# Attention and ternary FFN block: row sums of all kv heads taken from exponentials, and down products in seven parts in both passes

## The reference

```python
x = layernorm(x + attention(x, wq, wk, wv, wo))
x = layernorm(x + ffn(x, gate_t, up_t, down_t, gate_s, up_s, down_s))
```

## Time and profile before

| | us |
|---|---|
| median of 3 runs | 1789.99 (1787.49 to 1791.25) |
| the profiled execution | 1786.88 |
| its span | 1785.2 |

### The profile page before, as it was taken

The page is one execution under the profiler, slowest core; times in us unless marked ns, Lnnn a source line. Parts: engine busy times, 40 slices in busy tenths (PEclk is TensorE's granted clock), DMA queues, the critical chain, the costliest instruction groups (busy, mean ns, idle before and its releaser), DMA issues.

```text
span 1785.2 us, 26942 instructions
## 1 busy us (share of the span) xinstructions
PE 1743.6 (98%) x9840; PEld 849.1 (48%) x9840; DVE 1166.6 (65%) x2423; ACT 829.6 (46%) x1675; POOL 462.1 (26%) x813
## 2 busy tenths in 40 slices
PE   8999999999999999999999999999999999999998
PEld 4745564564455434444444444444444444444444
DVE  7997698488758764556544445646657666677456
ACT  6687667566646665365333433441332222231321
POOL 3475456454554652300000002203100000003103
PEclk9999999999999999999999999999999999999999
DMA  8564345234335797477544345558312112132302
GB/s 268 101 137 91 78 119 120 67 101 126 54 84 125 185 213 271 159 256 273 168 174 139 131 161 171 191 159 190 130 62 70 58 66 79 48 110 89 112 12 83
DMA packets 228516, 233.46 MB, mean 131 GB/s; under 512 B 183712, under 2 KB 184352, under 8 KB 228384
## 3 DMA queue, kind: packets, MB, share of 16 engines
q1 hardware_dynamic: 227520, 231.26, 44.6%
q10 hardware_dynamic: 864, 0.49, 0.1%
HBM read 122.78 MB, written 72.88 MB: 110 GB/s over the span
## 4 chain that ended last, share of the span: by engine, by line
PE 87%; DVE 6%; DMA 2%; issue 2%; ACT 1%; SPq 1%; POOL 1%; DVEq 0%; ACTq 0%; POOLq 0%
PE bank L1199 37%; PE bank L1084 18%; PE bank L1219 14%; PE bank L1232 7%; PE bank L1125 3%; PE bank L1100 3%; PE bank L1143 3%; PE bank L1158 1%; DVE bank L1450 1%; SPq L1818 1%; DMA att_parts<-att_spill 0%; PE bank L1104 0%; DMA p_tiles<-xT 0%; DVE max_parts L1461 0%; ACT p_tiles L1291 0%
## 5 line engine op out<-in xcount | busy, mean ns | idle before, releaser
L1199 PE MATMUL bank<-x_forms,weight_forms 128*128 128x512 f16 x3136 | 698.1, 379 | 4.0 <-DVE up_blocks L1610 1.6
L1199 PEld LDWEIGHTS bank<-x_forms,weight_forms 128*128 128x128 f16 x3136 | 306.1, 98 | 376.3 <-DVE up_blocks L1610 4.2
L1219 PE MATMUL bank<-down_forms 128*128 128x512 f16 (+1 forms) x1168 | 256.4, 376 | 0.0
L1715 POOL TENSOR_TENSOR acc<-acc,down_forms 128x1024 f32<-128x1024 f32 x16 | 39.2, 2456 | 696.8 <-DVE acc L1645 696.8
L1291 ACT ACTIVATE p_tiles<-bank 128x512 f32<-128x512 f32 (+1 forms) x352 | 184.2, 567 | 62.0 <-PE bank L1125 57.4
L1084 PE MATMUL bank<-wq_parts,xT_parts 128*128 128x256 f16 x1536 | 202.9, 274 | 8.5 <-DVE wq_parts L1406 8.1
L1450 DVE CUSTOM_DVE_ANT_0 bank<-bank,cmask 128x512 f32<-128x512 f32 (+2 forms) x320 | 179.4, 606 | 42.3 <-PE bank L1100 41.7
L1645 DVE TENSOR_TENSOR acc<-bank,acc 128x512 f32<-128x512 f32 x188 | 128.3, 688 | 103.1 <-PE bank L1219 64.6
L1219 PEld LDWEIGHTS bank<-down_forms 128*128 128x128 f16 x1168 | 114.3, 98 | 134.6
L1084 PEld LDWEIGHTS bank<-wq_parts,xT_parts 128*128 128x128 f16 x1536 | 149.5, 98 | 55.1 <-DVE wq_parts L1406 8.1
L1310 ACT ACTIVATE bank<-bank,row_max 128x128 f32<-128x128 f32 (+3 forms) x256 | 130.1, 511 | 78.6 <-DVE row_max L1450 74.6
(11 more groups left out here) (136 smaller groups left out, 2076.2 us busy)
## 6 DMA issues: line engine op xcount, KB each, us to landing
weight_forms_spill<-weight_forms SPq DMA_DIRECT2D x28, 896.0 KB, 4.8
weight_forms<-weight_forms_spill SPq DMA_DIRECT2D x28, 896.0 KB, 4.6
x_forms_spill<-x_parts SPq DMA_DIRECT2D x56, 256.0 KB, 2.6
w_page<-gateT SPq DMA_DIRECT2D x28, 512.0 KB, 5.3
w_page<-upT SPq DMA_DIRECT2D x28, 512.0 KB, 4.3
w_page<-downT SPq DMA_DIRECT2D x28, 512.0 KB, 3.7
att_spill<-att_made SPq DMA_DIRECT2D x64, 128.0 KB, 2.2
down_forms<-x_spill SPq DMA_DIRECT2D x16, 512.0 KB, 3.4
```

The costliest lines, as they stand in the source:

```text
L1199: t = nc.tensor.matmul(strassen[bank_set(use)][to][:, :], w_form[:, use % 4, A_FORMS[a_form], k * P:(k + 1) * P], xF[:, :, B_FORMS[b_form] ...
L1219: t = nc.tensor.matmul(to[:, 0:cols.stop - cols.start], hid_p[place_of(r)][:, k, a, i // 2 * P:(i // 2 + 1) * P], wd_p[place_of(r)][:, c, ...
```

## The change

1. `SUM_HEADS` takes in all groups: ACT takes exponentials and row sums of all 8 heads of a unit (512 instead of 256 in all), over rows twice as wide in the logarithm, which has two rounds instead of three. `sums`, `presum`, `sum_turn` and `att_scale` are gone. A bank of scores by query now always waits for ACT's `row_sum` before it is used again.
2. `mask_added` holds for query tile 0 alone: 32 matmuls with `cmask` and 32 reductions are replaced by 64 more of the custom operation.
3. `plain(n)` holds for the last four rounds of each pass alone: the first five groups of down products of pass 0 also use seven products. Their casts go into the form layout, and DVE makes the sums of weights in pass 0 too; `T3` overwrites a block that the store of the weights reads, and so waits for that store (`s_dst`). The ring has three places instead of four in pass 0.
4. One attention store instead of two for each unit and kv head.
5. `x1_store` is issued from ACT's queue, behind the norm.
6. The planner's costs are others (a hop for each engine, a list `AT_ONCE` of pairs that need no hop), and so is every number in `SHIFTS`.

```diff
-LN_STEPS = 3
+LN_STEPS = 2
-SUM_USES = [(i, h) for i, h in ROW_USES if h // REP == LOGGED]
-SUM_HEADS = [(i, h + k) for i, h in SUM_USES for k in range(ROW_HEADS[i])]
+SUM_HEADS = [(i, h + k) for i, h in ROW_USES for k in range(ROW_HEADS[i])]
-def mask_added(i, h):
-    return i == 0 or (i < MAX_MASKS and (i, h) not in SUM_USES)
+def mask_added(i):
+    return i == 0
 def row_end(u, i, h):
-    return ("row_sum", u, i, h + ROW_HEADS[i] - 1) if (i, h) in SUM_USES else ("row_max", u, i, h)
+    return "row_sum", u, i, h + ROW_HEADS[i] - 1
-DOWNS = [(q, m) for q in range(PASSES * ND) for m in range(PAIRS * NPR if ND <= q < PASSES * ND - 1 else 2 * PT)]
+DOWNS = [(q, m) for q in range(PASSES * ND) for m in range(PAIRS * NPR if q % ND < ND - 1 else 2 * PT)]
 def plain(n):
-    return n < NF or n % NF >= PLAIN
+    return n % NF >= PLAIN
 def room_after(n):
     p, r = divmod(n, NF)
-    if p == 0:
-        return DOWN_OF[r - 4] if r > 3 else None
-    return DOWN_OF[p * NF + min(r - 3, PLAIN - 1)] if r > 2 else p * ND - 1
+    if r > 2:
+        return DOWN_OF[p * NF + min(r - 3, PLAIN - 1)]
+    return p * ND - 1 if p else None
 SHIFTS = {
-    PE: {"down": -9, "max_tr": 2, "product": 4, "proj_out": -20, "proj_q": 54, "pv": 19, "sums": -1},
-    SC: {"att_hi": 9, "copy": -15, "exp": 18, "hid_hi": 15, "ln_exp": 11, "nat_hi": 150, "norm": -6, "row_sum": 128, "silu": 13,
+    PE: {"down": 20, "max_tr": 17, "product": 45, "proj_out": -9, "proj_q": 126, "pv": 12, "score_k": 5, "score_q": 13},
+    SC: {"exp": 328, "hid_hi": -4, "ln_exp": 32, "nat_hi": 381, "norm": 21, "row_sum": 156, "silu": 43, "split_hi": 54,
...
-                elif kind == "sums":
-                    for j in range(tiles):
-                        for h in range(REP):
-                            t = nc.tensor.matmul(bank[TRANS][h * HD:(h + 1) * HD, j * P:S], ones[:, :], p32[j][:, h, :],
-                                                 start=j == 0, stop=j == tiles - 1, tile_position=(0, h * HD))
...
+                elif kind == "x1_store":
+                    tile = which[0]
+                    on.wait_ge(s_norm, norm_n["norm", tile])
+                    e.dma_start(x1_dram[tile], row_of(tile)[:, :]).then_inc(s_x1[tile % 2], 16)
...
                 elif kind == "d_form":
-                    on.wait_ge(s_din[(n - NF) % 4], 16 * din_n(n))
+                    if n >= NF:
+                        on.wait_ge(s_din[(n - NF) % 4], 16 * din_n(n))
+                    else:
+                        for c in range(2):
+                            on.wait_ge(s_cast, cast_n["w_cast", 2, n, c])
+                        if form == "T3":
+                            on.wait_ge(s_dst[n % 4], 16 * (n // 4 + 1))
...
-                    for a in range(2):
-                        e.dma_start(att_dram[u // UNITS, :, :, a, gg, :].rearrange("t p c -> p t c"),
-                                    att_s[q % 2][:, a, :].rearrange("p (t c) -> p t c", t=NT)).then_inc(s_att[q % 2], 16)
+                    e.dma_start(att_dram[u // UNITS, :, :, :, gg, :].rearrange("t p a c -> p a t c"),
+                                att_s[q % 2][:, :, :].rearrange("p a (t c) -> p a t c", t=NT)).then_inc(s_att[q % 2], 16)
```

More of the change, by code:

```diff
@@ L279, in put @@
         rank += SHIFTS.get(engine, {}).get(kind, 0)
-        self.pieces[name] = (engine, rank, us, after, takes, frees, lands, moves)
+        self.pieces[name] = (engine, rank, us, after, takes, frees, HOP[engine] if lands is None else lands, moves)
     def close(self):
@@ L316, in close @@
             if moves:
-                queue = max(queue, now + us) + moves
+                queue = max(queue, now + ISSUES) + moves
                 lands = queue + LANDS - free[e]
@@ L327, in close @@
                 left[other] -= 1
-                seen = 0 if e == self.pieces[other][0] != SY else lands
+                seen = 0 if e == self.pieces[other][0] and (e != SY or name[0] == other[0] == "stack") and (name[0], other[0]) not in AT_ONCE else lands
                 may[other] = max(may[other], now + us + seen)
@@ L524, in output_done @@
     normed(plan, tile, [("residual", tile, 0), ("residual", tile, 1)], end)
-    put(SY, end + 7, .4, "x1_store", tile, moves=PAGE_MOVES, after=[("norm", tile)])
+    put(SC, end + 5, .4, "x1_store", tile, moves=STORE_MOVES, after=[("norm", tile)])
     for form in MADE[2:] if odd else MADE[:2]:
@@ L672, in ffn_plan @@
         if part < ND - 1:
-            put(VE, at + one / (1 if plain(rounds[0]) else 2), .72, "acc", q, m, after=[("down", q, m)] + room)
+            put(VE, at + one / (1 if plain(rounds[0]) else 2), .61, "acc", q, m, after=[("down", q, m)] + room)
         else:
```

311 lines of the change are left out of this document (122 added, 189 removed).

## The result

The change made the kernel faster by less than I forecast: 1780.84 us (1778.23 to 1784.55, median of 6) against 1790.80 of the kernel before on the same chip (1787.49 to 1794.08, 6), a ratio of 0.9946 with an interval of 0.9936 to 0.9957. The forecast was 1756, its range 1743 to 1773. The profiled execution has a span of 1778.2 us, 7.0 less than before. So some 49 us of TensorE (PE) work went, and 7 to 10 us of time.

What follows compares the result with a forecast made beforehand. PE was taken to bound the kernel nearly everywhere, by its sum of matmuls. From the profiled 1786.9 us, -49.1 + 13.5 + 2 + 2 gave 1755, stated as 1756 us, range 1743 to 1773.

Steps and rivals of the forecast that it cites:

- Removed, 49.1 us: PE work taken away: `sums` 28.3 us, masks of query tile 1 3.5 us, down products of pass 0 17.3 us.
- The floor of the first two units: Start of attention: ACT's row sums make PE wait, 17 us of waits in place of 3.5, so +13.5 us.
- Rival 2: More waits than the floor: ACT fed late, more in the remaining attention and pass 0; 1770 to 1778 us, chance 0.17.
- rival 3: First 140 us: bunched waits drop PE's clock five times, 8 us on top, 1763 us; chance 0.07.
- The rest of the attention: Attention behind unit 1: PE's waits can fall or rise, between -4 and +12 us; taken as +2 us.
- Pass 0, +2: FFN pass 0: DVE's added work, the lost ring place and `T3` cost +2 us, bounds 0 and +10.
- DVE's share: FFN pass 0: DVE's busy share was to rise to 70 to 77%.
- Pass 1: Second FFN pass: to be as long as before.
- Stores: `x1_store` moved to ACT's queue and fewer attention stores: nothing either way.

Runs made afterwards that it cites:

- sums_only: The change with plain down products in pass 0 again, its new order numbers kept; 1801.0 us, ratio 1.0058 to the kernel before.
- sums_ffn_old: The change with plain down products in pass 0 and the two passes' order numbers of before; 1791.0 us, ratio 1.0012.
- two_order2: Kernel before with seven down products in pass 0, a second buffer for the last x1 forms' stores and other order numbers for the passes; 1774.9 us.
- down_thin: Kernel before with seven down products in pass 0, whose adds there cover 32 of 512 columns; 1790.8 us, ratio 1.0005.
- ffn_old: The change with the order numbers of before for the two passes, attention keeping the new ones; 1792.2 us, ratio 1.0013.
- att_old: The change with the order numbers of before for attention and projections, the passes keeping the new ones; 1798.9 us, ratio 1.0049.
- down_only: Kernel before with the seven down products in pass 0 alone, order numbers of before; 1792.1 us, ratio 1.0016.
- down_shift: Kernel before with seven down products in pass 0 and the change's order numbers for the two passes; 1790.1 us, ratio 1.0005.
- three_places: Kernel before, plain down products kept, with three ring places instead of four in pass 0; 1793.0 us, ratio 1.0028.

## Why the prediction was wrong, step by step

The work removed was right; the new waits were not. The sum had 17.5 us of them (13.5 for the first two units, 2 for the rest of the attention, 2 for pass 0), and the runs have 41.6 in these three places (22.6, 10.7 and 8.3) and 3 in pass 1.

- **Removed, 49.1 us: right.** The matmuls are gone in that number, and the ledger's bare time fell by 51.6, of which some 2 us are its own error on `sums` (so the attention's waits below are up to 2 us too high).
- **The floor of the first two units: the step that missed most. The mechanism was there in part, the size was not.** "ACT ends at 141.4, PE at about 141", it said, with 4 us of idle on ACT. ACT was full, but only from 90 us on, and idled about 12 us before, 8.9 of them for row maxima; over 36 to 140 us it was busy for 90.54 of 104, or 87%, where over 95% was forecast, and the 44th product by key was over at 153 to 154 instead of 145. The term was +13.5 and it measured 22.6 (waits at the end of unit 2 from 7 to 30). A count of one engine's work gives a lower bound; the feed of that engine was the bound for its first 50 us. Rival 2 had this (ACT fed late, 12 us idle) and the right three places, but 15 us for them where 24 to 27 came, and its reason, a DVE at 93%, did not hold: DVE was busy for 71.23 of 90 us and waited itself.
- **The clock, rival 3: it happened three times, not five.** In the profiled execution PEclk fell at 50, 104 and 640 us, some 5 us in all by its low stretches, where before it fell once; these 5 us are in the waits of the other points. I had it as a rival instead of in the sum.
- **The rest of the attention, +2 with bounds of -4 and +12: right for twelve units, wrong for the end.** Units 3 to 14 brought 2.7 us of waits. The last two and the hand-over to the FFN brought 8 more, 10.7 in all, just inside the bounds; I had not looked at the end of the attention by itself. From 606 to 690 us PE now waits 2.2 us for `max_rows` and 1.7 for row sums, where it waited for neither before.
- **Pass 0, +2 with bounds of 0 and +10: the step that failed in kind.** It measured +8.3, within its bounds; the reasons that I gave were "nearer to pass 1, of this same pattern", the third ring place and `T3`. None of these is needed for it: `sums_only` has plain products, four places and no `T3` in pass 0, and the same 12 us of waits, where `sums_ffn_old` has 5 with the old order numbers. So that much waiting comes with the new numbers alone. In the change itself 3.6 us of PE's idle time are for adds of DVE (`acc`) and 4.6 for gate and up blocks, so that its 12 us have the same source is likely, but not shown. `two_order2` has 6 us with seven products in another order, and in the old order the seven products meet the late first adds, which pass 1 does not have (23 us). I had looked at DVE's share (forecast 70 to 77%, measured 71) and it did not matter, as `down_thin` shows for the old order.
- **Pass 1: 3 us more of waits, forecast none**, at the edge of what the ledger can tell.
- **Stores: nothing, right.**
- Together, by the ledger: -51.6 + 22.6 + 10.7 + 8.3 + 3 = -7.0, and the profiled execution is 6.9 us shorter. Of the miss of 25 us the first units were 9, the rest of the attention 9, pass 0 6 and pass 1 3, less 2.5 for the ledger's price of `sums`.
- **What I did not price at all was the order.** The change moves nearly every number of `SHIFTS`, and I took them for a given. They were worth 12 us in the passes and 18 in the attention (`ffn_old` and `att_old`, by their ratios against the change's), more than the gain that I was arguing about. `two_order2` shows what an order can do: its waits are nearly those of before (27 and 6 us), and so it keeps some 13 of the 17.3 us that its seven products save.

## What to carry to other kernels

Where one engine is 98% busy and lists are fixed, removing its work moves the question to the first dependencies that now arrive too late: look for the point at which a stage's buffers come free (here the last store of the stage before) and count back from it, before adding up shares of busy time. Narrowing an instruction to a few columns, with the order kept, tells an engine's load from the order in one run: if the time stays, the load of that engine is not the matter. And judge a rewrite and its order together: the same seven products were worth nothing in one order and 17 us in another.

## What the runs showed of the hardware

The clock adds to the longer waits. Behind an idle of 5.80 us the stretches of `down_only` have PEclk 0.53 and then 0.62; behind 2.75 us it fell too, and in the change, around the idle of 2.60 us at 104, it was 0.50 over four whole us in which PE was busy for 3.27. The level is 1.2 GHz where the row says 0.50. By the low stretches behind them, these three idles cost 1.4 to 2 us more than their length. Not every idle of that size did. Behind the 2.34 us at 782.80 in `down_only` the clock stayed at 2.4 GHz; in `down_shift` an idle of 2.77 us at 407.39 left it there, where in the kernel before the same idle at 406.7 made it fall; and in `three_places` it stayed there even behind 3.40 us. A timeline row and two stretches of `three_places`:

```profile
858.66 8.79 PE L1199 MATMUL bank<-x_forms,weight_forms 128*128 128x512 f16 x40 [3.40 <-DVE gate_blocks L1611]
```

```profile
856.00:860.00 4.00, 1.34 (x7) 0.66 (x8) 3.10 (x5) 4.00 (x7) 0.00 (x0) 1.00 0.00 0
860.00:864.00 4.00, 4.00 (x20) 1.81 (x19) 0.69 (x1) 2.48 (x5) 0.00 (x0) 1.00 0.77 199
```

So in these traces the length of an idle alone does not tell whether the clock falls. The Trainium skill (TensorE: Matmul & The Clock Gate, Why this matters for your kernels) warns of idle gaps between bursts, as the clock then drops. By that rule, the traces agree for three of these six.
